# An AdaLN model with a retention layer on one core: the conditioning no longer a stage of its own

## The reference

```python
mod = (_silu(L0_c) @ L0_wmod).reshape(16, 6, 1, -1)      # 16x256 @ 256x1536
sa, ca, ga, sb, cb, gb = (mod[:, n] for n in range(6))
ga = (2 * (ga >= 0) - 1) * jnp.maximum(jnp.abs(ga), 0.25) # gb likewise
h = _layernorm(x) * (1 + ca) + sa
x = x + ga * _L0_attn_ref(h, ...)
    # sig = sigmoid(h @ W_ret + b_ret); ret = running 0.5*sig_t + 0.5*ret
    # h = layernorm(h + ret); out = layernorm(h + gelu(h @ W1 + b1) @ W2 + b2)
h = _layernorm(x) * (1 + cb) + sb
x = x + gb * _L0_ffn_ref(h, ...)      # router and 16 experts
# layer 1: the same pattern with its own six vectors, another mixer and MLP
```

## Time and profile before

| | us |
|---|---|
| median of 3 runs | 3710.34 (3709.44 to 3711.82) |
| the profiled execution, its own time | 3706.35 |
| its span, first to last instruction | 3704.5 |
| PE busy | 3314.4 (89%) |
| DVE busy | 2605.8 (70%) |
| ACT busy | 1995.5 (54%) |
| POOL busy | 1267.6 (34%) |
| mean granted TensorE clock, as a share of 2.4 GHz | 0.946 |

### The profile page before, as it was taken

How to read it: one execution, slowest core, us unless ns; L and a number is a source line. 1 busy time by engine, 2 the same in 40 slices (tenths; PEclk the granted TensorE clock), 3 DMA queues, 4 the chain that set the end, 5 groups by cost and what they waited for, 6 DMA issues and landing times.

```text
span 3704.5 us, 66522 instructions
## 1 busy us (share of the span) xinstructions
PE 3314.4 (89%) x25034; PEld 2787.3 (75%) x25034; DVE 2605.8 (70%) x5973; ACT 1995.5 (54%) x3890; POOL 1267.6 (34%) x1081
## 2 busy tenths in 40 slices
PE   3999999999991199999999448999999999999999
PEld 1888888888881189999999336777777777777788
DVE  4677777777777844444444378888888888888864
ACT  2666666666650055555555235555555555555544
POOL 1233333333320256666665333222222222222210
PEclk7999999999995599999999669999999999999999
DMA  5132322222111234444443355555555555555541
GB/s 188 64 107 101 105 94 91 73 73 81 53 42 55 56 99 101 92 102 103 101 96 74 85 103 118 116 120 120 121 122 121 117 121 120 121 121 117 107 100 41
DMA packets 745478, 365.05 MB, mean 99 GB/s; under 512 B 551354, under 2 KB 695974, under 8 KB 745030
## 3 DMA queue, kind: packets, MB, share of 16 engines
q1 hardware_dynamic: 716486, 317.78, 34.6%
q0 software_dynamic: 28672, 43.02, 6.4%
HBM read 223.73 MB, written 136.97 MB: 97 GB/s over the span
## 4 chain that ended last, share of the span: by engine, by line
PE 80%; DVE 10%; ACT 3%; issue 3%; POOL 1%; DMA 1%; SPq 0%; POOLq 0%; DVEq 0%; ACTq 0%
PE bank L1278 10%; PE bank L1262 10%; PE bank L1880 9%; PE bank L1894 9%; PE bank L755 8%; PE bank L736 8%; PE bank L1851 7%; PE bank L121 5%; PE bank L714 3%; PE bank L1862 3%; PE bank L1831 2%; DVE hits L1071 2%; ACT xh_ L505 2%; PE bank L1826 1%; PE bank L1860 1%
## 5 line engine op out<-in xcount | busy, mean ns | idle before, releaser
L1554 POOL TENSOR_TENSOR energies<-energies,energy 128x496 f32<-128x496 f32 x128 | 162.3, 1268 | 783.8 <-DVE energies L1720 783.8
L1202 DVE TENSOR_TENSOR hidden_low<-bank,hidden_high 128x512 fp32r<-128x512 f32 x256 | 176.9, 691 | 313.4 <-ACT hidden_high L1012 253.5
L1894 PE MATMUL bank<-l_w_high,l_hidden_low 128*128 128x256 f32 x1024 | 303.0, 296 | 40.4 <-DVE l_hidden_low L1782 40.4
L644 DVE TENSOR_TENSOR gT_low<-bank,gT_high 128x512 fp32r<-128x512 f32 x256 | 173.3, 688 | 229.1 <-ACT gT_high L550 229.1
L544 ACT ACTIVATE bank<-bank,b 128x512 f32<-128x512 f32 x256 | 170.2, 665 | 273.2 <-PE bank L736 270.3
L1005 ACT ACTIVATE bank<-bank,fc_bias 128x512 f32<-128x512 f32 x256 | 170.2, 665 | 263.5 <-PE bank L1262 231.2
L755 PE MATMUL bank<-w_high,gT_low 128*128 128x256 f32 x1024 | 308.5, 301 | 0.8 <-DVE gT_low L644 0.8
L1851 PE MATMUL bank<-bandT,window 128*32 128x96 f32 x5632 | 271.4, 345 | 22.3 <-issue 21.1
L1894 PE MATMUL bank<-l_w_high,l_hidden_high 128*128 128x256 f32 x1024 | 289.9, 283 | 0.0
L1894 PE MATMUL bank<-l_w_low,l_hidden_high 128*128 128x256 f32 x1024 | 289.4, 283 | 0.0
L755 PE MATMUL bank<-w_high,gT_high 128*128 128x256 f32 x1024 | 289.3, 283 | 0.0
(11 more groups left out here) (298 smaller groups left out, 10587.8 us busy)
## 6 DMA issues: line engine op xcount, KB each, us to landing
bandT<-bands SPq DMA_DIRECT2D x352, 240.0 KB, 3.5
fc_full<-in_L_ffn_fc_wT SPq DMA_DIRECT2D x32, 1024.0 KB
bands<-zeros SPq DMA_DIRECT2D x22, 768.0 KB, 8.6
x<-in_L_attn_x SPq DMA_DIRECT2D x32, 512.0 KB, 6.3
moe_output<-zeros SPq DMA_DIRECT2D x32, 512.0 KB, 7.2
x_after_retention<-x SPq DMA_DIRECT2D x32, 512.0 KB, 3.0
moe_input_and_gates<-xn SPq DMA_DIRECT2D x32, 512.0 KB, 4.1
x<-x_after_retention SPq DMA_DIRECT2D x32, 512.0 KB, 5.3
```

The source lines that it names most:

```text
L644: v.tensor_tensor(t.gT.low[:, g % SLICES, :], K.banks[t.bank["expand", i, g, 0]][:, :], t.gT.high[:, g % SLICES, :], ALU.subtract).then_in ...
L1202: v.tensor_tensor(t.hidden.low[:, n % SLICES, :], K.banks[t.bank["expand", i, f, 0]][:, :], t.hidden.high[:, n % SLICES, :], ALU.subtract) ...
L1894: p = pe.matmul(K.banks[6 + ch // 2][:, left:left + D], x, w, start=False, stop=f == KF - 1 and j == 2 and ch % 2 == 1)
```

## The change

The conditioning has no stage any more, and there are three meetings instead of four. SyncE first loads the first condition, the first 512 columns of the first `wmod` (shift and scale of the first norm), the first tile of tokens, and the second condition; then the retention weights; then the rest of the conditioning's data, with the second tile of tokens between the two MLP weights. Ahead of the retention loop only the first product, its copy, one added one and the turn of four blocks remain. Everything else is made a step of the first tile: `ONCE_B` gives each a place, and each engine does it for i == 0 alone. The other five products go to banks 3, 4, 5, 6, 7. `load_rows` moves from place 30.76 to 31.05. The tiles `gT`, `x1`, `h2`, `xn`, `xnT`, `square`, `lg` of the retention now lie where the conditioning's tiles lay.

```diff
+MOD_BLOCKS = [[(0, 0), (0, 1)], [(1, 0), (1, 1), (1, 3), (1, 4)]]
+MOD_BANKS = (6, 3, 4, 5, 6, 7)
...
+def product_of_conditions(K, t0, pe, n):
+    s, bank = K.sem, MOD_BANKS[n]
+    l, n_of = divmod(n, K.NM // BANK)
+    K.free.take(pe, bank, *K.setup("vector", f"mod_copied{n}"))
+    for k in range(K.KD):
+        m = pe.matmul(K.banks[bank][0:K.B, :], t0.sc[l][:, k, :], t0.wm[l][:, k, n_of * BANK:(n_of + 1) * BANK], start=k == 0, stop=k == K.KD - 1)
+    m.then_inc(s("tensor_setup"), 1)
+
+def copy_product(K, t0, v, n):
...
+    v.wait_ge(*K.setup("tensor", f"mod_product{n}"))
+    v.tensor_copy(t0.mod[l][:, n_of * BANK:(n_of + 1) * BANK], K.banks[MOD_BANKS[n]][0:K.B, :]).then_inc(s("vector_setup"), 1)
+    v.wait_ge(*K.setup("vector", f"mod_copied{n}"))
...
-    "run": (21.25, 21.93), ... "load_rows": 30.76,
+    "run": (21.25, 21.93), ... "load_rows": 31.05,
...
+ONCE_B = [(20.6, "mod_products"), (22.0, "mod_copies"), (22.3, "take_mlp", 0), (30.9, "fields"), (30.95, "gain", 0, 2), (31.0, "rows", 0), (31.1, "bias"),
+          (31.6, "take_mlp", 1), (32.3, "columns_one"), (35.3, "gain", 0, 5), (37.3, "gain", 1, 2), (39.3, "gain", 1, 5), (39.35, "rows", 1)]
...
@@ retention_sync
+    e.dma_start(t0.cT[0][:, :, :], A["L0_cT"].rearrange("(k p) b -> p k b", p=P)).then_inc(s("cond0"), 16)
+    e.dma_start(t0.wm[0][:, :, 0:BANK], wm[0][:, :, 0:BANK]).then_inc(s("cond0"), 16)
+    load_x(0)
+    e.dma_start(t0.cT[1][:, :, :], A["L1_cT"].rearrange("(k p) b -> p k b", p=P)).then_inc(s("cond1"), 16)
     e.wait_ge(*K.setup("vector", "router_zero"))
     ... (the 14 transfers of the retention weights)
+    e.dma_start(t0.wm[0][:, :, BANK:], wm[0][:, :, BANK:]).then_inc(s("cond_more"), 16)
+    e.dma_start(t0.wm[1][:, :, :], wm[1]).then_inc(s("cond_more"), 16)
+    for n, name in enumerate(("L0_attn_W1", "L0_attn_W2")):
+        e.dma_start(t0.full[n][:, :, :], A[name].rearrange("(k p) n -> p k n", p=P)).then_inc(s(f"mlp_in{n}"), 16)
+        if n == 0:
+            load_x(1)
+    (four vectors, then the loop; load(0) and load(1) now send only zeros)
+        elif name == "rows" and i == 0:
+            (n,) = args
+            e.wait_ge(*K.setup("vector", f"rows{n}"))
+            e.dma_start((K.row0_dram, K.row1_dram)[n], t0.rows[n]...).then_inc(s("rows_sent"), 16)
         elif name == "load_rows" and i % t.PER == 0:
+            if b == 0:
+                e.wait_ge(s("rows_sent"), 16)
@@ retention_scalar
+    for l, loaded in enumerate((32, 16)):
+        e.wait_ge(s(f"cond{l}"), loaded)
+        e.activation(t0.th[l][:, :, :], t0.cT[l][:, :, :], ACT.Tanh, scale=0.5).then_inc(s("scalar_setup"), 1)
+        if name == "take_mlp" and i == 0:      # the high part of W1 or W2
@@ retention_vector
+    for l in range(2):
+        silu(K, t0, v, c, l)
+    copy_product(K, t0, v, 0)
+    v.tensor_scalar(field(K, t0, 0, 1), field(K, t0, 0, 1), 1.0, None, ALU.add).then_inc(s("vector_setup"), 1)
+    copy_columns(K, v, 0)
     v.wait_ge(s("b_weights"), 16 * (10 + C))
-    (three instructions that make b2, now the step "bias")
+        if name == "mod_copies" and i == 0:
+            for n in range(1, 6):
+                copy_product(K, t0, v, n)
+        ... fields, columns_one, gain, rows, take_mlp (the low part), bias
@@ retention_tensor
+    product_of_conditions(K, t0, pe, 0)
+    pe.wait_ge(*K.setup("vector", "field0"))
+    turn_fields(K, t0, pe, 0)
     pe.wait_ge(s("b_weights"), 16 * (10 + C))
     pe.wait_ge(*K.setup("vector", "ret_bias"))
+        if name == "mod_products" and i == 0:
+            pe.wait_ge(*K.setup("vector", "c_silu1"))
+            pe.wait_ge(s("cond1"), 16)
+            pe.wait_ge(s("cond_more"), 32)
+            for n in range(1, 6):
+                product_of_conditions(K, t0, pe, n)
+        elif name == "columns_one" and i == 0:
+            pe.wait_ge(*K.setup("vector", "field1"))
+            turn_fields(K, t0, pe, 1)
 ...(expand with f == 0 waits for mlp_low0, contract with f == 0 for mlp_low1 and bias)
```

More of the change, by code:

```diff
@@ L222, in conditioning_pool @@
-def conditioning_pool(K, t, e):
-    s = K.sem
[L224 to L231, removed]
-    s = K.sem
[L233 to L238, removed]
@@ L292, in conditioning_tensor @@
[L292 to L309, removed]
+    t.rows = [K.tile(ctx, "rows0", [K.B, 4, K.D]), K.tile(ctx, "rows1", [K.B, 4, K.D])]
@@ new lines, in copy_product, with turn_fields @@
+def copy_product(K, t0, v, n):
+    s = K.sem
+    l, n_of = divmod(n, K.NM // BANK)
+    v.wait_ge(*K.setup("tensor", f"mod_product{n}"))
+    v.tensor_copy(t0.mod[l][:, n_of * BANK:(n_of + 1) * BANK], K.banks[MOD_BANKS[n]][0:K.B, :]).then_inc(s("vector_setup"), 1)
+    v.wait_ge(*K.setup("vector", f"mod_copied{n}"))
+def turn_fields(K, t0, pe, l):
+    s = K.sem
+    K.free.take(pe, 7, *K.setup("vector", f"cols{l}"))
+    for n, (_, i) in enumerate(MOD_BLOCKS[l]):
+        for k in range(K.KD):
+            m = pe.transpose(K.banks[7][:, (2 * n + k) * K.B:(2 * n + k + 1) * K.B], t0.mod[l][:, i * K.D + k * P:i * K.D + (k + 1) * P], K.ident[0:K.B, 0:K.B])
+    m.then_inc(s("tensor_setup"), 1)
@@ L402, in retention_tiles, with later_retention_tiles, retention_sync @@
     return t
-def retention_sync(K, t, e):
+def later_retention_tiles(K, ctx, t):
+    C, D = t.C, K.D
+    t.gT = K.split_tile(ctx, "gT", [P, SLICES, t.GT])
+    t.x1, t.h2, t.xn = (K.ring(ctx, n, 2, [P, C, D]) for n in ("x1_", "h2_", "xn"))
+    t.xnT = K.tile(ctx, "xnT", [P, C, D])
+    t.square, t.lg = K.tile(ctx, "square", [P, D]), K.ring(ctx, "lg", 2, [P, P])
+def retention_sync(K, t, t0, e):
     s, A = K.sem, K.A
@@ L613, in retention_vector @@
         row = t.rows[i // t.PER % 2]
-        if name == "stats_in":
+        if name == "mod_copies" and i == 0:
+            for n in range(1, 6):
+                copy_product(K, t0, v, n)
+        elif name == "fields" and i == 0:
+            for l, n in ((0, 4), (1, 1), (1, 4)):
+                v.tensor_scalar(field(K, t0, l, n), field(K, t0, l, n), 1.0, None, ALU.add).then_inc(step, c.up())
+            v.wait_ge(step, c.n)
+            v.tensor_copy(t0.work[:, 2, :], field(K, t0, 1, 4)).then_inc(s("vector_setup"), 1)
+        elif name == "columns_one" and i == 0:
+            copy_columns(K, v, 1)
+        elif name == "gain" and i == 0:
+            bounded_gain(K, t0, v, c, *args)
+        elif name == "rows" and i == 0:
+            make_rows(K, t0, v, c, *args)
+        elif name == "take_mlp" and i == 0:
+            (n,) = args
+            parts = (t.w1, t.w2)[n]
+            v.wait_ge(*K.setup("scalar", f"mlp_high{n}"))
+            v.tensor_tensor(parts.low[:, :, :], t0.full[n][:, :, :], parts.high[:, :, :], ALU.subtract).then_inc(s("vector_setup"), 1)
+        elif name == "bias" and i == 0:
+            v.tensor_copy(t.b2[:, :, :], t.b2_full[:, :, :]).then_inc(step, c.up())
+            v.wait_ge(step, c.n)
+            v.tensor_scalar(t.b2_full[:, :, :], t.b2_full[:, :, :], t.pick[:, 0:1], None, ALU.mult).then_inc(step, c.up())
+            v.wait_ge(step, c.n)
+            v.scalar_tensor_tensor(out=t.b2[:, :, :], in0=t.b2[:, :, :], scalar=t.pick[:, 1:2], in1=t.b2_full[:, :, :],
+                                   op0=ALU.mult, op1=ALU.add).then_inc(s("vector_setup"), 1)
+        elif name == "stats_in":
             v.wait_ge(s(f"x_in{i % 2}"), 16 * (i // 2 + 1))
@@ L742, in retention_tensor @@
             if f == 0:
+                pe.wait_ge(*K.setup("vector", "mlp_low1"))
+                pe.wait_ge(*K.setup("vector", "bias"))
                 for n in range(2):
@@ L1908, in build @@
         K.token_share = K.tile(ctx, "token_share", [P, K.T // P])
-        with ExitStack() as kept:
-            with ExitStack() as part:
-                t0 = conditioning_tiles(K, part, kept)
-            with ExitStack() as part:
-                t1 = retention_tiles(K, part, t0)
+        with ExitStack() as part:
+            t1 = retention_tiles(K, part)
+            with ExitStack() as first:
+                t0 = conditioning_tiles(K, first)
+            later_retention_tiles(K, part, t1)
         with ExitStack() as part:
```

205 lines of the change are left out of this document (95 added, 110 removed).

## The result

The changed kernel takes 3677.32 us (median of 4 runs, 3673.8 to 3686.08) where the kernel before takes 3709.89; the ratio is 0.9917, 95% interval 0.9897 to 0.9938. The forecast was 3680.3. The profiled execution took 3673.8, its span is 3672.0. Run again beside later versions, the same kernel had a ratio of 0.9918 (0.9905 to 0.9932).

The account below looks back on a forecast made before the run. The chain of waits bounds the kernel before 87.42 us, TensorE after it. -40.65 + 9.25 + 1.0 + 0.4 = -30.0 takes 3706.35 to 3676.35; with 4.0 up to the median, 3680.3, range 3673 to 3692.

Parts of the forecast that it names:

- Part 1: Start-up to the first statistics: stats_in(0) starts at 11.5 instead of 52.15, a gain of 40.65 us.
- Part 2: stats_in(0) to stats_mid(0): five products on TensorE's path lengthen it from 22.13 to 31.4 us, +9.25.
- half clock: Rival: the five products run at 1.2 GHz after TensorE's wait, 17.0 us, 8.1 more; 3688.4 us; chance 0.12.
- The tie of VectorE and TensorE at stats_mid(0): In tile 0, VectorE is free at 42.8, about when TensorE's path arrives at 42.85; 42.9 taken.
- Part 3: stats_mid(0) to the first MLP product: stays 13.14 us, so the MLP starts at 56.0.
- columns_one: Eight turns between expand(0, 0) and expand(0, 1) cost 1.0 us on TensorE.
- Part 4: VectorE's remaining small work inside the MLP of tile 0 costs 0.4 us; 13 us without any cover.
- The sign that the prediction named: Prediction called wrong if TensorE has holes of over 1 us between 60 and 95.
- No gain: Rival: something other than TensorE paces the layer and the start is made up later; 3710 us; chance 0.03.
- slower: Rival: new addresses of gT, x1, h2, xn make each tile pay; 1.3 us a tile gives 3720; chance 0.04.
- Loads early or late: Rival at start-up: weights at 10.8 with x(1) at 20, 3677; either 4 us later, 3684; chance 0.05.
- VectorE: Rival: VectorE becomes the bound in tile 0; 3693 us all uncovered, 3687 for half; chance 0.10.

Follow-up runs that it names:

- old load order: Changed kernel with the conditioning's data and MLP weights loaded ahead of the first tokens and retention weights again, steps kept in the first tile; 3686.24 us.
- the products ahead: Changed kernel with the five products and their copies ahead of the first tile's statistics, new load order kept; 3684.28 us.
- the split with tile 1 first: The split version, plus tile 1 of the tokens loaded ahead of the rest of the conditioning's weights; 3673.78 us, ratio 0.9898.
- the products in the gaps: Against the split with tile 1 first: products 4 and 5 between modulate(2) and first MLP product, VectorE steps reordered, load_rows at 33.5; 3667.01 us, ratio 0.9888.
- the split version: Changed kernel with products 1, 2 behind modulate(1), 3 to 5 behind retain(1, 1), MLP weight split in two steps, gain(1, 2) moved; 3673.64 us.

## Why the prediction was right, step by step

- **Part 1** gave 40.65, measured 40.63. The products' start (5.99, forecast 5.9), their length and the columns held; no wait for the weights is in the timeline, ret_bias (11.46) follows the columns' copy at once.
- **Part 2** gave +9.25, measured 32.73 - 22.13 = +10.60. The wait for x(1), norm_in(1) and bank 3 was there with its numbers: readable at 22.24 (22.6), tanh's end 28.57 (28.9). The term that was mis-sized is the products' length: 8.9 forecast, 10.44 measured. The rival "half clock" came true for a part: the clock fell for some 3.5 us, not for all, so neither 8.9 nor 17 us came. Where the clock stayed, behind 1.20 and 1.69 us idle (old load order), the 20 matmuls took 8.74. Idle times of 2.17 and 2.21 us in two executions of the changed kernel cost 1.7 over that, 4.18 us with the products doubled 1.5 over twice that, and 3.47 us with the moved gain 2.8. So my reading of the earlier trace rows, that an idle time of under 2.94 us keeps the level, was the wrong part: a shorter one was followed by a fall, and with the products ahead one of 2.95 at the same place was too. Nor does a length near it decide. The same product of two later versions, the split with tile 1 first and the products in the gaps, behind 2.38 and 2.27 us:

```profile
36.00 3.68 PE L781 MATMUL bank<-h1T,w_ret 128*128 128x512 f32 x4 [2.38 <-DVE mod L227]
```
```profile
36.07 1.98 PE L782 MATMUL bank<-h1T,w_ret 128*128 128x512 f32 x4 [2.27 <-DVE mod L227]
```

The first ran at the lower level, the second at the higher. The Trainium skill, "TensorE: Matmul & The Clock Gate", Part 1, says that the chip judges the engine's activity on a count that runs freely and doesn't restart with the kernel; by it, like idle times can end differently, and these rows agree. The tie of VectorE and TensorE at stats_mid(0) held, at 44.25.
- **Part 3** gave 0, measured 12.47 instead of 13.14, as GpSimd's second small step (L487) took 0.20 us instead of the 1.03 before, and the low part 0.16 more. columns_one was 0.66 instead of 1.0, and the 18 MLP matmuls took 5.87 instead of the 7.17 of the earlier trace rows: together 1.3 us better than the sum, by the moment at which the clock returned.
- **Part 4** gave 0.4. gain(1, 2) cost 1.25, shown by moving it alone; another 0.25 was lost between contract(0, 5) and the first sent tile and went with it. The sign that the prediction named, a hole of over 1 us on TensorE between 60 and 95, did appear (1.24). The step that failed is the length of what follows the gain: L684 took 1.59 instead of 0.69. Moved by 2 us, it fell on GpSimd's hT_low, which ran from 83.42 for 3.57 us, where the two of them in the kernel before missed each other by 0.4. gain(0, 5) and gain(1, 5) cost nothing, as said.
- **Sum**: 40.63 - 10.60 + 0.67 + 0.63 - 1.25 - 0.25 = 29.83, the same as SyncE's rows; the forecast was 30.0. Errors of +1.35 (part 2), -2.3 (part 3 with columns_one) and +1.1 (part 4) cancelled, which was luck. The 3.0 us between the forecast and the median say nothing about the steps, since layer one alone varies by more; 2.7 us of the 32.5 in the spans lie there, and no term of the prediction stands for them.
- **The rivals.** "No gain" and "slower" are out: 32.10 us a tile in both. "Loads early or late" didn't happen: the weights weren't waited for and x of tile 1 was 0.4 early. "VectorE" was true for 1.25 us here, and became the bound only when everything was put behind stats_mid(0). The products ahead and the old load order, each undone alone, give back 9.5 and 10.0 of the 29.8; the rest wasn't divided further, and the two weren't undone together.

## What to carry to other kernels

A step moved off a start-up chain is only hidden if the engine's queue has nothing urgent behind it: doubling the step tells at once whether it is (here the whole length came through). Look for the engine's own gaps further down and put the pieces there; on TensorE it may pay twice, since with work in the gap ahead of a dense stretch the clock was up when that stretch began (one execution, 2.94 us for twelve matmuls instead of 5.42; not separated from chance). And when dealing out buffers for a moved step, ask who frees each one: here a bank, not data, was what the first product waited for.

## What was not expected of the hardware

The clock's return doesn't follow the start of the dense work one to one. With the MLP starting at 50.50, 51.24 and 56.72 the clock was at 2.4 GHz at 60.0, 60.5 and 60.0; a start at 50.55 in the split version, whose only edit against the first of these is x(1)'s place among the loads, had it at 54.0. With the gain moved and with the old load order it came back before the MLP (56.0 and 62.5, while TensorE waited) and fell again within 1 us of its start. So savings of 3 and 5.5 us ahead of the MLP were worth 0.57 and 2.83. What decides it was not settled.

From one execution to another layer one's share differs by up to 10 us with the same instructions: from its first transfer to the end 1616.4 in the changed kernel's profile, 1626.0 in that with the moved gain. The stretches of the two, aligned at that transfer, first the changed kernel:

```profile
2455.63:2655.63 200.00, 193.33 (x1751) 157.76 (x1752) 168.18 (x331) 110.45 (x225) 59.94 (x49) 0.99 0.56 119
```

and the one with the moved gain:

```profile
2458.13:2658.13 200.00, 194.24 (x1755) 158.22 (x1755) 166.16 (x332) 108.38 (x220) 58.73 (x48) 0.97 0.59 119
```

The lower mean clock goes with the longer time, also over the runs (0.953 at 3673.8, 0.946 at 3686.08); which of the two causes the other was not tried.

VectorE and GpSimd slow each other. L684, which reads two tiles in SBUF, took 1.59 us instead of 0.69 beside hT_low in all seven traces with gain(1, 2) in its place, and 0.69 in all four where the gain was moved and the two didn't meet; hT_low took 3.57 instead of 2.54 where they met. GpSimd's root of tile 1 took 1.79 instead of 1.01 where L684 began while it ran, and ended 0.08 us after L684 (26.51 against 26.43 with the moved gain). The Trainium skill, "SBUF — State Buffer", Who interferes with whom, says that the two share one pair of ports, that a VectorE instruction with two inputs in SBUF contends with a GpSimd instruction that reads SBUF, and that the pair is an exclusive lock. The rows fit it; that the ports are the cause no run here separates.
